# Two mixture-of-experts layers: residual sum and norm on the sorted rows, finished rows scattered back, in place of storing the expert outputs and gathering them

## What is computed

```
# L1: every token goes to its best expert
expert_idx = argmax(xf @ Wr.T + br)
y[t] = relu(x[t] @ W1[e] + b1[e]) @ W2[e] + b2[e]          # width 512 inside
# L2: the same with gelu, but an expert takes its first 80 tokens only;
# the others get 0 from this part. The result is scaled by the gate's probability
pos = position of the token among its expert's tokens;  keep = pos < 80
out[t] = keep * gate_prob[t] * y[t]
```

## Time and profile before

| | |
|---|---|
| time, median of 3 runs | 1622.76 us (1622.22 to 1625.02) |
| the profiled execution | 1620.42 us, its span 1618.6 us |
| mean granted TensorE clock | 0.922 |
| busy | PE 80%, DVE 72%, POOL 51%, ACT 45% |
| L1's mixture | from about 1010 to 1121 us |
| L2's mixture | from about 1310 to 1383 us |

### The profile page before, as it was taken

The page is one execution under the profiler, slowest core; times in us unless marked ns, Lnnn a source line. Parts: engine busy times, 40 slices in busy tenths (PEclk is TensorE's granted clock), DMA queues, the critical chain, the costliest instruction groups (busy, mean ns, idle before and its releaser), DMA issues.

```text
span 1618.6 us, 41193 instructions
## 1 busy us (share of the span) xinstructions
PE 1291.4 (80%) x15406; PEld 876.6 (54%) x15406; DVE 1168.8 (72%) x2520; ACT 725.8 (45%) x1486; POOL 824.2 (51%) x1030
## 2 busy tenths in 40 slices
PE   7989869886878868779999788893888883898871
PEld 4556536556645547456666455681555543465540
DVE  6977858984688856568898577434788853798875
ACT  3544435544555544234444354250556521355555
POOL 4543357761377644435453364326557624456654
PEclk9999989997999989879999999795999987899995
DMA  9000000000000000000000000123000012000000
GB/s 340 1 1 1 0 0 0 0 1 22 0 1 0 0 1 14 0 7 1 0 0 1 1 0 3 44 56 132 1 0 1 0 42 35 3 0 2 0 1 26
DMA packets 19559, 29.95 MB, mean 19 GB/s; under 512 B 4291, under 2 KB 16323, under 8 KB 18714
## 3 DMA queue, kind: packets, MB, share of 16 engines
q1 hardware_dynamic: 17562, 24.97, 4.5%
q0 software_dynamic: 1920, 3.94, 1.4%
HBM read 23.91 MB, written 4.98 MB: 18 GB/s over the span
## 4 chain that ended last, share of the span: by engine, by line
PE 41%; DVE 23%; issue 15%; POOL 13%; ACT 6%; DMA 1%; POOLq 1%; DVEq 0%; ACTq 0%; SPq 0%
PE ps L333 32%; DVE maxima L430 6%; PE ps L453 4%; DVE arena L432 4%; PE ps L825 3%; POOL inv_norm L905 3%; ACT arena L440 3%; DVE heads_out L765 2%; POOL arena L910 2%; POOL arena L525 2%; DVE sq_sum L1039 1%; POOL arena L1940 1%; DVE gate L1795 1%; POOL arena L2228 1%; POOL rstd L371 1%
## 5 line engine op out<-in xcount | busy, mean ns | idle before, releaser
L333 PE MATMUL ps<-arena 64*64 64x64 f32 (+5 forms) x7921 | 381.8, 279 | 22.0 <-ACT arena L1222 4.7
L333 PEld LDWEIGHTS ps<-arena 64*64 64x64 f32 (+4 forms) x7921 | 236.2, 134 | 152.7 <-issue 122.3
L525 POOL TENSOR_TENSOR arena<-arena,w_const 128x1024 f32<-128x1024 f32 x96 | 182.3, 1901 | 151.7 <-DVE arena L755 66.7
L430 DVE TENSOR_REDUCE maxima<-ps 128x16 f32<-128x1024 f32 (+1 forms) x144 | 158.5, 1101 | 56.5 <-PE ps L333 52.6
L440 ACT ACTIVATE arena<-arena 128x1024 f32<-128x1024 f32 (+1 forms) x144 | 138.5, 962 | 127.9 <-DVE arena L432 127.0
L453 PE MATMUL ps<-w_const,arena 128*128 128x128 f32 x1024 | 144.1, 283 | 50.8 <-ACT arena L440 34.0
L905 POOL TENSOR_TENSOR inv_norm<-sq_floor,minus_half 128x16 f32<-128x16 f32 x32 | 121.9, 3810 | 86.4 <-DVE sq_floor L1042 86.2
L432 DVE TENSOR_TENSOR arena<-ps,maxima 128x1024 f32<-128x1024 f32 (+1 forms) x144 | 159.3, 1106 | 4.9
L447 ACT COPY arena<-ps 128x1024 f32<-128x1024 f32 (+1 forms) x144 | 131.4, 912 | 56.2 <-PE ps L453 55.7
L453 PEld LDWEIGHTS ps<-w_const,arena 128*128 128x128 f32 x1024 | 116.3, 144 | 74.0 <-ACT arena L440 44.2
L371 POOL TENSOR_TENSOR rstd<-var_eps,minus_half 128x1 f32<-128x1 f32 x144 | 80.5, 570 | 140.7 <-DVE var_eps L873 100.4
(11 more groups left out here) (317 smaller groups left out, 2649.7 us busy)
## 6 DMA issues: line engine op xcount, KB each, us to landing
experts<-in_pack_moe SPq DMA_DIRECT2D x2, 4180.0 KB, 20.3
w_fa<-in_pack_fa SPq DMA_DIRECT2D x2, 1024.0 KB, 11.2
moe_in<-state SPq DMA_DIRECT2D x2, 1024.0 KB, 5.4
w_a<-in_pack_a SPq DMA_DIRECT2D x1, 1824.0 KB, 18.0
moe_out<-arena SPq DMA_DIRECT2D x5, 256.0 KB, 3.5
w_fg<-in_pack_fg SPq DMA_DIRECT2D x2, 537.0 KB, 11.9
ctxT<-in_ctxT SPq DMA_DIRECT2D x1, 1024.0 KB, 7.4
out<-state SPq DMA_DIRECT2D x4, 256.0 KB, 2.3
```

What stands on the lines that cost most here:

```text
L333: return nc.tensor.matmul(o, lhsT, rhs, start=start, stop=stop, skip_group_check=True)
L430: nc.vector.reduce_max(mx, sc, X_AXIS).then_inc(signal["max_ready"], 1)
L525: nc.gpsimd.tensor_tensor(keys_wide(s).rearrange("p (b h t) -> p b h t", b=SEQS, h=8), key8(s).rearrange("p (b t) -> p b t", b=SEQS).unsqu ...
```

## The change

- Sum and norm are done on the sorted rows. A sorted row's input (gathered for the expert anyway) is the token's state, so state + bias + expert output, bn_stats and bn_aggr can be taken there. L1: DVE adds the gathered row and the expert's b2 right after each fetch (`base`, one 128x128 add for each of 23 tiles), adds the PSUM result for four tiles at once (`summed`), and takes statistics (`measured`, `set_variance`). POOL turns variance into scale and bias (`set_inverse`: power, then a product), ACT applies them (`norm`), nine tiles behind its relu.
- POOL then scatters the finished rows to DRAM with an indirect DMA for each sorted tile, to one of two tables by turns (`moe_back`). The scatter of tile i waits for its norm and for the landing of scatter i - 2, which went to the same table. Pads go to rows behind the tables. Both tables are set to zero at the start of the program (four DMAs of 1 MB on SP), so that each token's row is in one of them and zero in the other.
- SP loads both tables back, each in two halves (`load_back`), and DVE adds the two and writes the state, four adds of 128x512.
- The buffer of an output tile is used again twelve tiles later: `base(i)` on DVE waits for the landing of scatter i - 12.
- L2: one gather of 80 rows for each expert, one transpose each; bias, scaling and sum on the expert's 80 rows, norm in sets of two experts, 8 scatters. The norm of the plain state, for the tokens that no expert takes, is made at the start (16 bn_stats, 16 bn_aggr, a power of 128x16, 16 ACT operations), and added where the token was dropped. The slot numbers and the gate's value (as three bf16 parts) go through the same matmul.
- L1's one-hot transposes, their copies and the bias matmuls are gone. `experts` has the bias rows in it now: 9256 columns in place of 8360. The bias matmuls ahead of L2's attention use another PSUM bank, and some semaphores are merged.

```diff
         moe_in = nc.dram_tensor("moe_in", (TILES * P, D), F32).ap()
-        moe_out = nc.dram_tensor("moe_out", (SORTED * P, D), F32).ap()
+        moe_back = [[nc.dram_tensor(f"moe_back{m}{k}", ((TILES + 1) * P, D), F32).ap() for k in range(2)]
+                    for m in range(2)]
...
+        def set_inverse(pool, k, first, n, rows):
+            pool.wait_ge(gs["g_var"], k + 1)
+            nc.gpsimd.tensor_tensor(g_rstd[0:rows, first:first + n], g_var[0:rows, first:first + n],
+                                    minus_half[0:rows, 0:n], ALU.pow).then_inc(gs["g_rstd"], 1)
+            pool.wait_ge(gs["g_rstd"], k + 1)
+            nc.gpsimd.tensor_tensor(g_bias[0:rows, first:first + n], g_minus_mean[0:rows, first:first + n],
+                                    g_rstd[0:rows, first:first + n], ALU.mult).then_inc(gs["g_bias"], 1)
+
+        def normed(out, x, j, rows=P):
+            return nc.scalar.activation(out, x, ACT.Identity, bias=g_bias[0:rows, j:j + 1],
+                                        scale=g_rstd[0:rows, j:j + 1])
+
+        def load_back(sp, use, order, buffers):
+            for n, k in enumerate(order):
+                sp.wait_ge(returned[k], 16 * (RETURNED1[k] + (EXP // 2) * use))
+                for h in range(2):
+                    sp.dma_start(buffers[k][:, h * 2 * GT:(h + 1) * 2 * GT].rearrange("p (t d) -> p t d", d=D),
+                                 moe_back[use][k][h * 2 * GT:(h + 1) * 2 * GT, :].rearrange("(t p) d -> p t d", p=P))\
+                        .then_inc(back_loaded[2 * n + h], 16)
 
...
+        FIRST_BACK1 = [SORTED % 2, (SORTED + 1) % 2]
...
+            def return_rows(first, n):
+                for i in range(first, first + n):
+                    pool.wait_ge(ms["m_normed"], i + 1)
+                    if i >= 2:
+                        pool.wait_ge(returned[i % 2], 16 * (i // 2))
+                    nc.gpsimd.indirect_dma_start(moe_back[0][i % 2],
+                                                 bass.IndirectOffsetOnAxis(m_scatter32[:, i:i + 1], 0),
+                                                 out_of(i), None).then_inc(returned[i % 2], 16)
...
+            fetch_rows(0)
+            fetch_rows(1)
+            fetch_rows(2)
+            for j in range(3, SORT_GROUPS):
+                pool.wait_ge(ms["m_up"], 4 * j - 11)
+                if j + 1 == SORT_GROUPS:
+                    set_inverse(pool, 0, *SETS1[0], P)
+                fetch_rows(j)
+            for k, (first, n) in enumerate(SETS1):
+                return_rows(first, n // 2)
+                if k + 1 < len(SETS1):
+                    set_inverse(pool, k + 1, *SETS1[k + 1], P)
+                return_rows(first + n // 2, n - n // 2)
...
-            for q in range(GROUPS):
-                s, b = onehot_bank[q]
-                for k in range(4):
-                    t = 4 * q + k
-                    last = nc.tensor.transpose(ps[s][0:EXP, b, k * P:(k + 1) * P],
-                                               m_onehot[:, t * EXP:(t + 1) * EXP], ident)
-                last.then_inc(ms["m_turned"], 1)
...
+            def norm(i):
+                act.wait_ge(gs["g_bias"], SET_OF1[i] + 1)
+                normed(out_of(i), out_of(i), i).then_inc(ms["m_normed"], 1)
...
+            def base(i):
+                if i % 4 == 0:
+                    dve.wait_ge(rows_moved[i // 4], 16 * tiles_in(i // 4))
+                if i >= 12:
+                    dve.wait_ge(returned[i % 2], 16 * ((i - 12) // 2 + 1))
+                nc.vector.tensor_tensor(out_of(i), m_sorted[:, i * P:(i + 1) * P],
+                                        part("moe1", "experts")[:, EXPERT_BODY:][:, ds(bias_at[i], D)], ALU.add)\
+                    .then_inc(gs["g_based"], 1)
...
+            def summed(k):
+                first, n = SETS1[k]
+                dve.wait_ge(ms["m_down"], first + n)
+                dve.wait_ge(gs["g_based"], first + n)
+                s, b = [(0, 0), (1, 0)][k % 2]
+                nc.vector.tensor_tensor(out_of(first, n), out_of(first, n), bank(s, b, 0, n * D), ALU.add)\
+                    .then_inc(gs["g_sum"], 1)
...
+                base(i)
+            for i in range(3, SORTED + 3):
+                if i < SORTED:
+                    fetch(i)
+                    base(i)
+                if i % 4 == 2 and i >= 6 or i == SORTED + 2:
+                    summed((i - 3) // 4)
+                if i % 4 == 3 and i >= 7 or i == SORTED + 2:
+                    measured((i - 4) // 4 if i < SORTED + 2 else len(SETS1) - 1)
+                if i % 4 == 0 and i >= 8 or i == SORTED + 2:
+                    k = (i - 5) // 4 if i < SORTED + 2 else len(SETS1) - 1
+                    set_variance(dve, k, *SETS1[k], P)
             for g in range(GROUPS):
-                dve.wait_ge(tile_done, 2 + 16 * ph + 4 * g)
-                dve.wait_ge(rows_moved[g], 2 * 4 * 16)
-                nc.vector.tensor_tensor(g_acc, m_acc[:, g * GT:(g + 1) * GT], m_gathered[:, g * GT:(g + 1) * GT],
-                                        ALU.add).then_inc(gs["g_sum"], 1)
-                dve.wait_ge(gs["g_sum"], g + 1)
-                group_norm_vector(dve, 0, g)
-
+                dve.wait_ge(back_loaded[g // 2], 16)
+                dve.wait_ge(back_loaded[2 + g // 2], 16)
+                nc.vector.tensor_tensor(state[:, 4 * g:4 * g + 4, :].rearrange("p a n -> p (a n)"),
+                                        m_gathered[:, g * GT:(g + 1) * GT], m_second[:, g * GT:(g + 1) * GT],
+                                        ALU.add).then_inc(tile_done, 4)
 
         carve = carver()
...
+            def return_expert(e):
+                pool.wait_ge(ms["m_normed"], SORTED + e + 1)
+                if e >= 2:
+                    pool.wait_ge(returned[e % 2], 16 * (RETURNED1[e % 2] + e // 2))
+                nc.gpsimd.indirect_dma_start(moe_back[1][e % 2],
+                                             bass.IndirectOffsetOnAxis(c_scatter32[:, e:e + 1], 0),
+                                             c_out[:, e * D:(e + 1) * D], None).then_inc(returned[e % 2], 16)
+
+            LAST2 = len(SETS2) - 1
+            for k, (first, n) in enumerate(SETS2[:LAST2]):
+                set_inverse(pool, FIRST2 + k, TILES + first, n, CAP)
+                return_expert(first)
+                if k + 1 == LAST2:
+                    set_inverse(pool, FIRST2 + LAST2, TILES + SETS2[LAST2][0], SETS2[LAST2][1], CAP)
+                return_expert(first + 1)
+            for e in range(SETS2[LAST2][0], EXP):
+                return_expert(e)
 
         def moe2_tensor(ph):
             pe = tensor_engine
...
+            act.wait_ge(gs["g_bias"], BASE2 + 1)
+            for t in range(TILES):
+                last = normed(c_base[:, t * D:(t + 1) * D], state[:, t, :], t)
+            last.then_inc(cm["c_based"], 1)
...
+                if e >= 4:
+                    norm(e - 4)
...
+            place = c_place16.rearrange("p (t a e) -> p t a e", t=TILES, a=5)
+            left = c_best
+            for k in range(3):
+                if k < 2:
+                    then(nc.vector.tensor_copy(c_best16[k], left))
+                    then(nc.vector.tensor_tensor(c_rest[k], left, c_best16[k], ALU.subtract))
+                    left = c_rest[k]
+                else:
+                    then(nc.vector.tensor_copy(c_best16[k], left))
+                nc.vector.tensor_tensor(place[:, :, 2 + k, :], tiled(c_onehot), per_tile(c_best16[k]), ALU.mult)
...
+                nc.vector.tensor_tensor(out, ps[1][0:CAP, e % 2, 0:D],
+                                        part("moe2", "experts")[0:CAP, bias2:bias2 + D], ALU.add)\
+                    .then_inc(cm["c_out"], 1)
+                dve.wait_ge(cm["c_out"], e + 1)
+                return nc.vector.scalar_tensor_tensor(out=out, in0=out, scalar=c_p[:, e:e + 1],
+                                                      in1=c_rows[:, e * D:(e + 1) * D], op0=ALU.mult, op1=ALU.add)
+
...
+            dve.wait_ge(cm["c_based"], 1)
             for g in range(GROUPS):
-                dve.wait_ge(tile_done, 2 + 16 * ph + 4 * g)
-                dve.wait_ge(rows_moved[g], MOVED[g] + 16 + 4 * 16)
-                for k in range(4):
-                    t = 4 * g + k
+                dve.wait_ge(back_loaded[g // 2], 32)
+                for t in range(4 * g, 4 * g + 4):
                     last = nc.vector.scalar_tensor_tensor(
...
+            sp.wait_ge(tables_ready, 1)
+            for m in range(2):
+                for k in range(2):
+                    sp.dma_start(moe_back[m][k][0:TILES * P, :].rearrange("(t p) d -> p t d", p=P),
+                                 shT[0][:, :].unsqueeze(1).broadcast_to([P, TILES, D])).then_inc(blanked, 16)
```

More of the change, by code:

```diff
@@ L1841, in program @@
         carve = carver()
[L1842 to L1854 removed]
+        g_x, g_xT = carve(GT), carve(GT)
@@ L1870, in groups @@
-        def groups(eng, body):
-            with eng.Fori(0, GROUPS - 1) as g:
```

(15 more changed lines are left out.)

400 lines of the change are left out of this document (185 added, 215 removed).

## The result

The changed kernel takes 1629.97 us (median of 19 runs, 1622.18 to 1636.38), the kernel before 1622.76 (median of 19, 1616.68 to 1629.59): ratio 1.004, 95% interval 1.0026 to 1.0054. It is **slower by some 6.5 us** where the prediction had 6.7 us less. The profiled run took 1632.23 us.

What follows compares the result with a forecast made beforehand. No engine is full (PE nearest at 80%); the tails behind the last `down`, chains of 16 gathers on POOL, count. L1 +2.5, L2 -9.2 and elsewhere 0 sum to -6.7 us: 1616 us against the median, range 1609 to 1628.

Steps and rivals of the forecast that it cites:

- L1, (a) start of the loop: L1 ahead of the expert loop: one more small DVE step, PE loses one-hot work; no change.
- L1, (b) the loop: L1's expert loop: waits for scatter landings add 1.35 us a set for nearly three sets, +3.9; last `down` at 1092.0.
- The ring: L1's loop: variance, POOL's power, scatter, landing and DVE's steps through `base` take 9.4 us where PE wants 8.05.
- L1, (c) and (d): L1's end: eleven scatters, 3.25 us for two, then four table halves back; twelfth tile 1118.7 against 1116.25, L1 +2.5 us.
- The rivals that lived on a landing of 2.2 or 3.2 us: Scatters land later in DRAM: 2.2 us gives -2 us, chance 0.17; 3.2 us gives +11, chance 0.12.
- The cheaper rival: Landing 1.2 us, 0.3 after a wait, 80-row DMAs 0.65: L1 -1, L2 -11, in all -12, 1611; chance 0.14.
- L2: the total: L2's mixture: dropped-token steps and adds end at 1367.7 against 1376.87, so L2 -9.2 us.
- PE's clock: Pauses of 1 to 2 us in L1's loop drop the granted clock to 0.5: -3 us, 1620; chance 0.10.
- Elsewhere 0: Outside the mixtures: blanking and larger weights on SP's queue cost 0, or 13 us if their cover were gone.
- forecast -6.7: Whole kernel: L1 +2.5 and L2 -9.2 make -6.7 us; chance of -10 to -4.5 is 0.47.
- The rival for the other side: Scatters land in 3.2 us and `base` holds PE up in every set: L1 +17, L2 -6, +11, 1634; chance 0.12.

Runs made afterwards that it cites:

- pattern two: Chips or occasions where no update of PE comes late in the mixtures; the unaltered changed kernel takes 0.9978 and 0.9982 of before there.
- the pause that moved the hole: Changed kernel, L1's gathers of tiles 8 to 11 waiting for up 3, the next for up 5, 7 and 9: 1.0016, 0.9988 and 1.001 of before.
- pattern one: Chips or occasions where updates of PE come late in the mixtures; the unaltered changed kernel takes 1.004 and 1.0038 of before there.
- L1 old: Kernels with L1's mixture of before; with L2's mixture of after 0.9945 of before, with 21 fillers in L2 as well 0.99 to 0.9954.
- Six buffers: Changed kernel with six buffers of four output tiles in L1 in place of three: 1614.76 us, 0.9961 of before.
- first profile: First measurement of the unaltered changed kernel against before, chip not on record: 1629.97 us, 1.004.
- L2-only kernel: Changed kernel with L1's mixture of before and two tables blanked in place of four: 1611.54 us, 0.9945 of before.
- chip 12: Here the second measurement of the unaltered changed kernel: 1617.91 us, 0.9978 of before.
- seven more fillers: L1's mixture of before, L2's of after, 21 PE fillers in place of 14 ahead of L2's first turn: 0.9927, 0.9935, 0.99 and 0.9954 of before.

## Why the prediction was wrong, point by point

**L1, (a) start of the loop, "No change": failed on the chip of the measurement.** It costs 7.6 us there (third fetch 22.9 against 15.3 us). The step looked at clock and gathers, and both were right: on pattern two it is 15.2 to 15.3. It did not count that the loop's start now runs beside 16 gathers in a row where before has 12, and that PE's releases come late beside them on some chips. For the gathers' part in it speak the pause that moved the hole and the six traces of pattern one, where every late update falls beside an indirect DMA of POOL or within 2.8 us of the last one's end. Why only some chips have it stays open. Open too is what makes the lateness long: before has gathers beside its first `down` as well, and its updates are at most 1.2 us late. The length of the row and the new `base` adds of DVE were not tried apart.

**L1, (b) the loop: mechanism right, size off.** The ring runs as described, with the waits at L2189 for `moe_back`, but four times (at tiles 12, 14, 18 and 22, 11.6 us), where the sum took "nearly three" sets. Within pattern two the last `down` is 62.7 us after the first gather against 55.0 to 56.1 with L1 old: +7.0, forecast +3.9. Six buffers give 5.9 of it back, so each of four sets costs 1.5 us, near the forecast 1.35: the term that was too small is how often the ring comes round. On pattern one the loop loses a further 2.3 us (49.8 against 47.4 from third fetch to last `down`).

**L1, (c) and (d): right, with some luck.** Pairs of scatters 3.0 to 3.1 us apart (3.25 forecast), drain 27.2 us (26.7). Two misses cancel in it: in the first profile the loads back start 16.9 us after the last `down` (forecast 17.8) and take 10.5 us to the fillers (forecast 8.9 to the twelfth tile). The rivals that lived on a landing of 2.2 or 3.2 us fall: `base` goes on 1.4 to 1.9 us after the scatter that it waits for has left POOL, once 2.9, and in the drain the next scatter but one starts 2.0 us after it (1120.56 to 1122.59). The cheaper rival falls as well.

**L2: the total right, partly by luck.** -8.6 against -9.2. The last `down` comes 2.7 us later, forecast 0.2, since the granted clock falls to 0.50 behind the pause ahead of the first `turn`. That is the rival *PE's clock*, in the other mixture. The drain is 18.7 us, forecast 19.7, and the fillers, which the forecast left as they were, are 1.0 shorter: two gains that hide most of it.

**Elsewhere 0: right** (L2-only kernel).

**The sum.** Pattern two: L1 +5.8 (89.7 against a mean of 83.9), L2 -8.9 (57.0 against 65.9, for which only the first profile of before stands): -3.1, measured -3.6 and -2.9. Pattern one: L1 +13.2 (99.9 against the mean 86.7 of 86.1 and 87.4), L2 -8.7: +4.5, measured +6.5 and +6.2; some 2 us of that stay unexplained. The forecast -6.7 missed by 3 for the ring and by 7.5 more for the late releases. The rival for the other side had the right sign for a wrong reason: slow landings, where it was late releases of PE.

The reading hinges on one detail of the page: matmul ends are modelled. The Trainium skill (Perfetto Trace Analysis, Tensor Engine Instruction) says that PE's end is computed from the instruction's size and that the semaphore update comes behind it, outside the reported window. The trace agrees: on chip 12, in L1's loop of the changed kernel, the 46 recorded updates of PE stand 0.01 to 0.02 us behind the modelled ends. Against that, the update of `up(2)` in the first profile stands 7.8 us behind (1051.64 and 1059.41).

## What to carry to other kernels

Where PE, ACT and DVE hand work to each other every microsecond, suspect long rows of POOL's indirect DMAs in that stretch; here they are harmless on four chips and go with a loss of 10 us on two others. No cure was found: the pause moved the hole and cost 3 to 4 us on pattern two, and a loop that runs several handovers ahead was not tried. A result near 0.4% depends on the chip or the occasion as well: measure the same program a second time elsewhere before the cause is sought in the code, and compare kernels only within one pattern. When a buffer is freed by a DMA's landing, count how often the wait comes round, not only what one costs; and seven more fillers in place of a pause of 1.1 to 1.5 us were worth 3 us on pattern two.

## What was unexpected in the hardware

The same program took 1617.9 and 1617.8 us on two chips and 1630.3 on another, while before lay between 1620.1 and 1625.2 on all six. On three of the seven occasions, updates of PE's semaphores came 0.6 to 8.6 us after the modelled end of the matmul, always in the mixtures beside indirect DMAs of POOL or just behind them; several came 0.1 us apart (1059.32, 1059.41 and 1059.51). POOL went on at its pace of 1.25 us a gather meanwhile. In the thirteen profiles of pattern two no recorded update of PE, ACT or DVE in the whole kernel is more than 0.6 us late.
